# A fused two-layer graph kernel on one core: start-up loads spread over other queues and no longer held back

## The chip, the cores and the metric

The kernel runs on one core of a Trainium2 chip. The metric is device time in microseconds (us) of one execution; the time before is the median of 3 runs.

## What is computed

There are 128 graphs of 128 nodes with 128 features. Layer 0 is a relational graph convolution, of which the fast path of this kernel computes the self-loop relation; layer 1 is a message passing over the same adjacency. Each is followed by a residual addition and a layer norm.

```python
# layer 0, the relation with id 1 (adj_t is adj with nodes swapped)
h = x @ W_loop.T
g = h @ Wg_loop.T
vals = (h + b_loop) * sigmoid(g + bg_loop)
x1 = layernorm(x + relu(onehot(adj_t == 1) @ vals))
# layer 1, relation 1
y = (adj == 1) @ x1 @ weight[0] + bias
out = layernorm(x1 + y)
```

The drawn adjacency has values 0 and 1 only. A general path, which is taken when another value is found, is in the program and is not executed with these inputs.

## The kernel before, in words

The 128 graphs are worked in 32 groups of four. All of a group's tiles are 128 partitions by 512 columns, so one transfer of `x` or of `x_t` for a group is 256 KB, and one transfer of `adj` or `adj_t` for a pair of groups is 512 KB. The program is written engine by engine, with semaphores between them; each engine works through its own list in order.

For group q the steps are:

- **project(q)** on TensorE (line 381): four 128x256 matmuls give `h` and `g` side by side. Each is executed as two passes, so the trace shows eight instructions. They add to bank `hg_ps`, into which ScalarE has first written the bias (`seed`, line 515). For group 0 half of the bias is written by VectorE (line 638).
- **gates(q)** on ScalarE (line 524): sigmoid of `g`. **values(q)** on VectorE (line 727): `h` times gate.
- **loop_sum(q)** on TensorE (line 393): adjacency times `vals`; `first_sum(q)` on VectorE (line 735) adds `x` after the relu, and `first_stats` (line 742) takes the statistics.
- A chain of nine small VectorE operations (lines 665 to 691) makes the reciprocal root; GpSimd then normalises (lines 325 and 333) into `x1`.
- **messages(q)** (line 411) and **message_weights(q)** (line 432) on TensorE, `second_sum` and its statistics on VectorE, the output scaling on ScalarE (line 551), and the store from SyncE.

TensorE's list in step t is project(t), loop_sum(t-1), message_weights(t-5), messages(t-4). VectorE's list in step t is second_sum(t-5) and its statistics, the chain for t, values(t), first_sum(t-1), and the two statistics.

Before the first group there is a start-up. `w_loop_both` (`W_loop` and its transpose) and `wg_loop_t` are loaded, and TensorE multiplies them (line 370, "the fold") so that `h` and `g` come from one product of `x_t` with the 128x256 weight `w_gate`; VectorE copies the product out (line 641, `weights_ready`). Four matmuls on a constant tile `warm` run ahead of the fold (line 367) and two behind it (line 372). VectorE prepares the layer 1 weight from `const_sb` in seven small operations, `message_weight()` (lines 647 to 656). After the sixth, `w1_mid` reaches 3, which is what TensorE's small matmul at line 441 waits for; that matmul stands between project(1) and loop_sum(0) in TensorE's list.

The loads come from three queues. ScalarE's queue has the two loop weights alone. SyncE's queue has `wg_t`, then `xt_sb` and `x_sb` in turn, six buffers of each. GpSimd's queue has the gate bias, the constants, and all of the adjacency, four pairs of each kind. The hold-backs in the lists of SyncE and GpSimd are these:

```python
sp.wait_ge(xt_in[0], 16)      # line 266, ahead of x_t of group 2
sp.wait_ge(xt_in[1], 16)      # line 268, ahead of x of group 1
sp.wait_ge(adj_in[0], 16)     # line 270, ahead of x_t of group 3
pool.wait_ge(xt_in[1], 16)    # line 341, ahead of adjacency pair 1
```

Of the kernel before, what the change touches and what calls it, by code (L numbers as in the profile page):

```python
# [56 lines left out]
    return ((t - FIRST_CHAIN) // 2 + 1) * CHAIN_OPS  # L57


def build(nc, x, x_t, adj, adj_t, w_loop_both, wg_loop_t, gate_bias, consts,  # L60
          w_rel_t, wg_rel_t, b_rel, bg_rel, w_msgs, rel_ids, out):
    with ExitStack() as ctx:
        def sb(name, shape, dt):
# [2 lines left out]
        def sem(name):  # L66
            return ctx.enter_context(nc.semaphore(name))
# [72 lines left out]
        adjt_in = [sem(f"adjt_in{j}") for j in range(ADJ_RING)]  # L140
        out_st = [sem(f"out_st{j}") for j in range(OUT_RING)]
        fold_in = sem("fold_in")
        consts_in = sem("consts_in")
        bias_in = sem("bias_in")
        share_ready = sem("share_ready")
# [76 lines left out]
        def arrived(q, ring):  # L222
            return 16 * (q // ring + 1)
# [18 lines left out]
        def _(sp):  # L242
            def load_xt(q):
                if exists(q):
                    await_count(sp, hg_done, q - XT_RING + 1)
                    sp.dma_start(xt_sb[:, q % XT_RING, :], x_t[q]).then_inc(xt_in[q % XT_RING], 16)
# [12 lines left out]
                    sp.dma_start(out[q], out_sb[:, q % OUT_RING, :]).then_inc(out_st[q % OUT_RING], 16)  # L259

            sp.dma_start(wg_t[:, :], wg_loop_t).then_inc(fold_in, 16)
            load_xt(0)
            load_xt(1)
            load_x(0)

            sp.wait_ge(xt_in[0], 16)
            load_xt(2)
            sp.wait_ge(xt_in[1], 16)
            load_x(1)
            sp.wait_ge(adj_in[0], 16)  # L270
            load_xt(3)
            load_x(2)
            load_xt(4)
# [28 lines left out]
        def _(pool):  # L302
# [32 lines left out]
                            r[:, b:b + 1], n[:, b:b + 1], ALU.mult, ALU.add)  # L335
                    last.then_inc(x1_done, 1)

            pool.dma_start(gate_b[:, :], gate_bias).then_inc(bias_in, 16)
            pool.dma_start(const_sb[:, :], consts).then_inc(consts_in, 16)
            load_adj(0)  # L340
            pool.wait_ge(xt_in[1], 16)
            load_adj(1)
            load_adjt(0)
            load_adj(2)
# [17 lines left out]
        def _(pe):  # L362
# [5 lines left out]
            last.then_inc(marked, 1)  # L368
            pe.wait_ge(fold_in, 16 * 2)
            nc.tensor.matmul(aux_ps[:, 0:P], w_loop, wg_t[:, :], start=True, stop=True).then_inc(fold_done, 1)  # L370
            for _ in range(2):
                nc.tensor.matmul(msg_ps[:, :], warm[:, :], warm_wide, start=True, stop=True)
            pe.wait_ge(weights_ready, 1)
            pe.wait_ge(seeded_dve, 1)

# [9 lines left out]
            def loop_sum(q):  # L385
                if exists(q):
                    spot = q // 2 % ADJ_RING * 2 + q % 2
                    pe.wait_ge(adj_in[q // 2 % ADJ_RING], arrived(q // 2, ADJ_RING))
                    pe.wait_ge(vals_done, q + 1)

                    await_count(pe, s_done, q)
                    for b in range(GB):
                        last = nc.tensor.matmul(loop_ps[:, batch(b)], adj_sb[:, spot, batch(b)],  # L393
                                                vals[:, q % 2, batch(b)], start=True, stop=True)
                    last.then_inc(loop_done, 1)
# [104 lines left out]

        @block.scalar
        def _(act):
            act.dma_start(w_all[:, 0:2 * P], w_loop_both).then_inc(fold_in, 16)
            act.wait_ge(table_ready, 1)
            nc.scalar.activation(table[:, :], half[:, :], ACT.Sigmoid)

# [48 lines left out]
            def look(q):  # L555
                if exists(q):
                    spot = q // 2 % ADJ_RING
                    act.wait_ge(adj_in[spot], arrived(q // 2, ADJ_RING))

                    await_count(act, seen_done, q)  # L560
                    nc.scalar.activation(seen[:, :], adj_sb[:, 2 * spot + q % 2, :], ACT.Square, bias=half[:, 0:1],  # L561
                                         accum_out=seen_sum[:, q:q + 1]).then_inc(seen_done, 1)
# [64 lines left out]
        def _(dve):  # L627
# [4 lines left out]
            nc.vector.memset(stats[:, :, :, :].rearrange("p a c d -> p (a c d)"), 0.0)  # L632
            nc.vector.memset(ones[:, :], 1.0)
            nc.vector.memset(share[:, :], 1.0 / P).then_inc(share_ready, 1)

            dve.wait_ge(marked, 1)
            dve.wait_ge(bias_in, 16)
            nc.vector.tensor_copy(hg_ps[:, 0, 2:4, :], gate_b[:, None, :].broadcast_to([P, 2, 2 * P]))\  # L638
                .then_inc(seeded_dve, 1)
            dve.wait_ge(fold_done, 1)  # L640
            nc.vector.tensor_copy(w_all[:, 2 * P:3 * P], aux_ps[:, 0:P]).then_inc(weights_ready, 1)  # L641

            def message_weight():

# [158 lines left out]
                dve.wait_ge(odd_ready, 1)  # L803
                ts(odd[:, :], worst[:, :], W / 4 + 0.5, None, ALU.is_gt).then_inc(odd_ready, 1)

            message_weight()
            for t in range(GROUPS + 1):
                steps = chain(t)

                def step(n):  # L810
                    for _ in range(n):
                        next(steps, None)

                if exists(t - Z_LAG):
                    second_sum(t - Z_LAG)
                    step(1)
                    second_stats(t - Z_LAG, 0)
                    step(1)
                    second_stats(t - Z_LAG, 1)
                    step(2)  # L820
                else:
                    step(CHAIN_OPS)
                if exists(t):
                    values(t)
                step(1)
                if exists(t - LOOP_LAG):
                    first_sum(t - LOOP_LAG)
                    step(2)
                    first_stats(t - LOOP_LAG, 0)
                    step(1)  # L830
                    first_stats(t - LOOP_LAG, 1)
                step(CHAIN_OPS)
                if t == 1:
                    message_weight_end()
# [137 lines left out]
```

## Time and profile before

| | |
|---|---|
| median of 3 runs | 167.06 us (166.71 to 167.41) |
| the profiled execution, its own time | 167.7 us |
| its span (first to last instruction) | 166.0 us |
| TensorE matmul busy | 153.1 us, 92% of the span |
| VectorE busy | 145.5 us, 88% |
| ScalarE busy | 126.2 us, 76% |
| GpSimd busy | 79.9 us, 48% |
| DMA | 42.76 MB, mean 258 GB/s |

The profiled execution took 1.7 us more than its span, for what lies around it, and its own time is 0.64 us above the median. All times of single instructions in this document are of that execution, in us from the start of the span. In the rows PE is TensorE's matmul, PEld its weight load, DVE is VectorE, ACT ScalarE, POOL GpSimd and SP SyncE; a q behind the name means the engine's sequencer or its DMA queue. "x8" behind a row means eight instructions merged.

### The profile page before, as it was taken

Reading aid. Unit: us, or ns where it says so; the run is one execution under the profiler, and the core shown is the slowest. Engines: PE = TensorE matmul, PEld = TensorE weight load, DVE = VectorE, ACT = ScalarE, POOL = GpSimd, SP = SyncE. Lnnn points to the kernel's source line nnn. Section 1 sums busy time; section 2 is a strip of 40 time slices with the busy share of each in tenths; the row PEclk is TensorE's granted clock in tenths of the full one; section 3 lists DMA queues with packets and bytes.
Section 4 is the critical chain, followed back from the end, with each engine's and each line's share of the span. In section 5 each row is a group of like instructions: output and inputs, shape, how many; then the busy total and the mean of one; then the engine's idle time right before and its main releaser. Section 6 shows DMA issues by size and latency. Waiting matters only on the chain.

```text
span 166.0 us, 3902 instructions
## 1 busy us (share of the span) xinstructions
PE 153.1 (92%) x1068; PEld 141.9 (85%) x1068; DVE 145.5 (88%) x583; ACT 126.2 (76%) x287; POOL 79.9 (48%) x194
## 2 busy tenths in 40 slices
PE   6499899999999999999999999999999999998910
PEld 2278789999999999999999999999999999997910
DVE  1425999999999999999999999999999999999770
ACT  3318767679988888888888888899888887754670
POOL 4070456264737474747466464646374544446000
PEclk9999999999999999999999999999999999999996
DMA  4999999989598979798998979797979261131133
GB/s 123 332 300 315 396 399 396 391 281 321 153 300 288 380 222 348 275 310 308 285 348 245 374 224 381 211 371 206 370 243 360 31 226 39 41 117 63 67 124 139
DMA packets 18857, 42.76 MB, mean 258 GB/s; under 512 B 2112, under 2 KB 2368, under 8 KB 18832
## 3 DMA queue, kind: packets, MB, share of 16 engines
q1 hardware_dynamic: 13968, 25.24, 42.3%
q0 software_dynamic: 4720, 17.11, 33.8%
q8 instruction: 10, 0.16, 0.4%
q14 instruction: 15, 0.12, 0.2%
q10 hardware_dynamic: 144, 0.13, 0.2%
HBM read 34.08 MB, written 8.39 MB: 256 GB/s over the span
## 4 chain that ended last, share of the span: by engine, by line
PE 85%; DVE 5%; issue 3%; DMA 3%; ACT 1%; ACTq 0%; DVEq 0%; POOLq 0%
PE hg_ps L381 33%; PE msg_ps L411 16%; PE loop_ps L393 15%; PE y_ps L432 15%; DMA gate_b<-gate_bias_dram 3%; PE hg_ps L432 2%; PE hg_ps L428 2%; DVE s_sb L735 1%; ACT gate L524 1%; PE y_ps L428 1%; PE hg_ps L411 1%; ACT out_sb L551 1%; DVE stats L742 0%; DVE hg_ps L638 0%; DVE z_sb L753 0%
## 5 line engine op out<-in xcount | busy, mean ns | idle before, releaser
L381 PE MATMUL hg_ps<-w_all,xt_sb 128*128 128x256 f32 x256 | 63.3, 393 | 2.2 <-DVE w_all L641 2.2
L333 POOL TENSOR_SCALAR x<-s_sb,rstd,nmr 128x128 f32<-128x128 f32 x125 | 55.0, 452 | 3.5 <-issue 0.2
L381 PEld LDWEIGHTS hg_ps<-w_all,xt_sb 128*128 128x128 f32 x256 | 48.2, 198 | 8.9 <-DVE w_all L641 3.1
L515 ACT ACTIVATE hg_ps<-gate_b 128x1024 f32<-128x1024 f32 (+1 forms) x32 | 32.0, 1002 | 9.6 <-DVE vals L727 6.0
L551 ACT ACTIVATE out_sb<-z_sb,rstd 128x128 f32<-128x128 f32 x112 | 38.0, 392 | 0.3 <-DVE rstd L691 0.2
L325 POOL TENSOR_TENSOR nmr<-mean_neg,rstd 128x4 f32<-128x4 f32 x31 | 6.2, 201 | 63.6 <-DVE rstd L691 63.6
L393 PEld LDWEIGHTS loop_ps<-vals,adj_sb 128*128 128x128 f32 x256 | 33.3, 192 | 2.7 <-issue 1.3
L393 PE MATMUL loop_ps<-vals,adj_sb 128*128 128x128 f32 x256 | 33.9, 275 | 0.5 <-DVE s_sb L735 0.5
L411 PE MATMUL msg_ps<-adjt_sb,x 128*128 128x128 f32 x248 | 33.0, 276 | 0.0
L524 ACT ACTIVATE gate<-hg_ps 128x512 f32<-128x512 f32 x32 | 19.1, 596 | 17.0 <-PE hg_ps L381 16.8
L432 PE MATMUL y_ps<-w,msg_t 128*128 128x128 f32 x232 | 30.7, 275 | 0.0
L411 PEld LDWEIGHTS msg_ps<-adjt_sb,x 128*128 128x128 f32 x248 | 30.2, 192 | 0.1
L432 PEld LDWEIGHTS y_ps<-w,msg_t 128*128 128x128 f32 x232 | 28.2, 192 | 0.0
L727 DVE TENSOR_TENSOR vals<-hg_ps,gate 128x512 f32<-128x512 f32 x32 | 22.0, 689 | 6.0 <-ACT gate L524 5.0
L742 DVE BATCH_NORM_STATS2 stats<-s_sb 128x6 f32<-128x256 f32 x64 | 26.5, 426 | 0.3
L757 DVE BATCH_NORM_STATS2 stats<-z_sb 128x6 f32<-128x256 f32 x56 | 23.7, 427 | 0.0
L561 ACT ACTIVATE seen<-adj_sb,half 128x512 bf16<-128x512 f32 x32 | 22.8, 711 | 0.1
L735 DVE SCALAR_TENSOR_TENSOR s_sb<-loop_ps,x_sb 128x512 f32<-128x512 f32 x32 | 21.8, 682 | 0.0
L534 ACT ACTIVATE msg_t<-msg_ps 128x512 f32<-128x512 f32 x31 | 18.0, 580 | 4.0 <-PE msg_ps L411 4.0
L753 DVE TENSOR_TENSOR z_sb<-y_ps,x 128x512 f32<-128x512 f32 x28 | 19.1, 683 | 0.0
L308 POOL DMA_DIRECT2D adj_sb<-adj_dram x16 | 9.4, 588 | 4.9 <-DMA xt_sb<-x_t_dram 4.9
L315 POOL DMA_DIRECT2D adjt_sb<-adj_t_dram x16 | 8.7, 545 | 0.0
(66 smaller groups left out, 103.8 us busy)
## 6 DMA issues: line engine op xcount, KB each, us to landing
xt_sb<-x_t_dram SPq DMA_DIRECT2D x32, 256.0 KB, 6.3
x_sb<-x_dram SPq DMA_DIRECT2D x32, 256.0 KB, 6.4
adj_sb<-adj_dram POOLq DMA_DIRECT2D x16, 512.0 KB, 4.5
adjt_sb<-adj_t_dram POOLq DMA_DIRECT2D x16, 512.0 KB, 6.7
out<-out_sb SPq DMA_DIRECT2D x32, 256.0 KB, 3.9
const_sb<-consts_dram POOLq DMA_DIRECT2D x1, 192.0 KB, 5.0
w_all<-w_loop_both_dram ACTq DMA_DIRECT2D x1, 128.0 KB, 2.3
gate_b<-gate_bias_dram POOLq DMA_DIRECT2D x1, 128.0 KB, 4.9
```

What stands on the lines that cost most here:

```text
L333: last = nc.gpsimd.tensor_scalar(x1[:, q % X1_RING, batch(b)], s_sb[:, q % S_RING, batch(b)], r[:, b:b + 1], n[:, b:b + 1], ALU.mult, ALU.add)
L381: last = nc.tensor.matmul(hg_ps[:, q % 2, b, :], xt_sb[:, q % XT_RING, batch(b)], w_gate, start=False, stop=True, skip_group_check=True)
L393: last = nc.tensor.matmul(loop_ps[:, batch(b)], adj_sb[:, spot, batch(b)], vals[:, q % 2, batch(b)], start=True, stop=True)
L411: last = nc.tensor.matmul(msg_of(q)[:, batch(b)], x1[:, q % X1_RING, batch(b)], adjt_sb[:, spot, batch(b)], start=True, stop=True)
L432: last = nc.tensor.matmul(y_of(q)[:, batch(b)], msg_t[:, q % 2, batch(b)], w1[:, :], start=q < LAST, stop=True, skip_group_check=q >= LAST)
L515: nc.scalar.activation(hg_ps[:, q % 2, 0:graphs, :], gate_b[:, None, :].broadcast_to([P, graphs, 2 * P]), ACT.Copy).then_inc(seeded, 1)
L551: last = nc.scalar.activation(out_sb[:, q % OUT_RING, batch(b)], src, ACT.Copy, scale=r)
L561: nc.scalar.activation(seen[:, :], adj_sb[:, 2 * spot + q % 2, :], ACT.Square, bias=half[:, 0:1], accum_out=seen_sum[:, q:q + 1]).then_inc ...
L727: tt(vals[:, q % 2, :].rearrange("p (b n) -> p b n", b=GB), hg_ps[:, q % 2, :, 0:P], gate[:, q % 2, :].rearrange("p (b n) -> p b n", b=GB) ...
L735: stt(s_sb[:, q % S_RING, :], loop_ps[:, :], 0.0, x_sb[:, q % X_RING, :], ALU.max, ALU.add)\
L742: got = nc.vector.bn_stats(stats[:, (q + NORM1_LAG) % STATS_RING, p, :], s_sb[:, q % S_RING, 2 * p * P:2 * (p + 1) * P].rearrange("p (i n) ...
L757: got = nc.vector.bn_stats(stats[:, (q + STAT2_LAG) % STATS_RING, 2 + p, :], z_sb[:, q % Z_RING, 2 * p * P:2 * (p + 1) * P].rearrange("p ( ...
```

## The change

It does six things to the start-up and leaves the groups' work as it was.

1. The gate bias and the constants are loaded from ScalarE's queue, behind `W_loop`, and no longer from GpSimd's.
2. `w_loop_both` is split: `W_loop` (64 KB) on ScalarE's queue, its transpose (64 KB) second on SyncE's queue, with a semaphore of its own, `w_gate_in`, that TensorE waits for ahead of project(0).
3. GpSimd's queue has the adjacency alone. The first pair goes in two transfers of 256 KB, and the readers of group 0 wait for the first of them (`first_adj`).
4. All four hold-backs are taken out, so that twelve loads of `x_t` and `x` and seven of the adjacency are issued with nothing to wait for.
5. There are three `warm` matmuls behind the fold where there were two.
6. VectorE copies the folded weight ahead of its half of the bias, and `message_weight()` is moved from ahead of the groups to behind values(0).

```diff
             sp.dma_start(wg_t[:, :], wg_loop_t).then_inc(fold_in, 16)
+            sp.dma_start(w_all[:, P:2 * P], w_loop_t).then_inc(w_gate_in, 16)
             load_xt(0)
             load_xt(1)
             load_x(0)
-            sp.wait_ge(xt_in[0], 16)
             load_xt(2)
-            sp.wait_ge(xt_in[1], 16)
             load_x(1)
-            sp.wait_ge(adj_in[0], 16)
             load_xt(3)
...
-            pool.dma_start(gate_b[:, :], gate_bias).then_inc(bias_in, 16)
-            pool.dma_start(const_sb[:, :], consts).then_inc(consts_in, 16)
-            load_adj(0)
-            pool.wait_ge(xt_in[1], 16)
+            pool.dma_start(adj_sb[:, 0, :], adj[0, :, 0:W]).then_inc(first_adj, 16)
+            pool.dma_start(adj_sb[:, 1, :], adj[0, :, W:2 * W]).then_inc(adj_in[0], 16)
             load_adj(1)
...
-            for _ in range(2):
+            for _ in range(3):
                 nc.tensor.matmul(msg_ps[:, :], warm[:, :], warm_wide, start=True, stop=True)
+            pe.wait_ge(w_gate_in, 16)
             pe.wait_ge(weights_ready, 1)
             pe.wait_ge(seeded_dve, 1)
...
-            act.dma_start(w_all[:, 0:2 * P], w_loop_both).then_inc(fold_in, 16)
+            act.dma_start(w_all[:, 0:P], w_in).then_inc(fold_in, 16)
+            act.dma_start(gate_b[:, :], gate_bias).then_inc(bias_in, 16)
+            act.dma_start(const_sb[:, :], consts).then_inc(consts_in, 16)
...
+            dve.wait_ge(fold_done, 1)
+            nc.vector.tensor_copy(w_all[:, 2 * P:3 * P], aux_ps[:, 0:P]).then_inc(weights_ready, 1)
             dve.wait_ge(marked, 1)
             dve.wait_ge(bias_in, 16)
             nc.vector.tensor_copy(hg_ps[:, 0, 2:4, :], gate_b[:, None, :].broadcast_to([P, 2, 2 * P]))\
                 .then_inc(seeded_dve, 1)
-            dve.wait_ge(fold_done, 1)
-            nc.vector.tensor_copy(w_all[:, 2 * P:3 * P], aux_ps[:, 0:P]).then_inc(weights_ready, 1)
...
-            message_weight()
             for t in range(GROUPS + 1):
...
                 if exists(t):
                     values(t)
+                if t == 0:
+                    message_weight()
                 step(1)
```

In `loop_sum` on TensorE and in `look` on ScalarE, group 0 waits for `first_adj` and every other group for `adj_in` as before.

VectorE's list at the start, before the change; `hg_ps<-gate_b` is the bias, `w_all<-aux_ps` the folded weight, and the rows on `mid_stat`, `mid`, `b_mid` and `const_sb` are `message_weight()`:

```order
L638 COPY hg_ps<-gate_b 128x512 [waits bias_in,marked]
L641 COPY w_all<-aux_ps 128x128 [waits fold_done]
L647 BN_STATS mid_stat<-const_sb 128x6 [waits consts_in]
L648 BN_STATS mid_stat<-const_sb 128x6
L650 BN_AGGR mid<-mid_stat 128x2 [waits w1_mid]
L651 BN_AGGR mid<-mid_stat 128x2
L653 TENSOR_SCALAR b_mid<-const_sb,mid 128x128 [waits w1_mid]
L654 TENSOR_SCALAR const_sb<-const_sb,mid 128x128
L656 TENSOR_TENSOR b_mid<-b_mid,const_sb 128x128 [waits w1_mid]
L727 TENSOR_TENSOR vals<-hg_ps,gate 128x512 [waits gate_done] x2
```

The same stretch of the changed kernel:

```order
L643 COPY w_all<-aux_ps 128x128 [waits fold_done]
L647 COPY hg_ps<-gate_b 128x512 [waits bias_in,marked]
L734 TENSOR_TENSOR vals<-hg_ps,gate 128x512 [waits gate_done]
L654 BN_STATS mid_stat<-const_sb 128x6 [waits consts_in]
L655 BN_STATS mid_stat<-const_sb 128x6
L657 BN_AGGR mid<-mid_stat 128x2 [waits w1_mid]
L658 BN_AGGR mid<-mid_stat 128x2
L660 TENSOR_SCALAR b_mid<-const_sb,mid 128x128 [waits w1_mid]
L661 TENSOR_SCALAR const_sb<-const_sb,mid 128x128
L663 TENSOR_TENSOR b_mid<-b_mid,const_sb 128x128 [waits w1_mid]
L734 TENSOR_TENSOR vals<-hg_ps,gate 128x512 [waits gate_done]
```

The two copies have changed places, and the seven rows of `message_weight()` now stand between values(0) and values(1).

SyncE's list of loads at the start, before the change:

```order
L261 DMA wg_t<-wg_loop_t_dram 128x128
L246 DMA xt_sb<-x_t_dram 128x512 x2
L251 DMA x_sb<-x_dram 128x512
L246 DMA xt_sb<-x_t_dram 128x512 [waits xt_in0]
L251 DMA x_sb<-x_dram 128x512 [waits xt_in1]
L246 DMA xt_sb<-x_t_dram 128x512 [waits adj_in0]
```

The same stretch of the changed kernel:

```order
L263 DMA wg_t<-wg_loop_t_dram 128x128
L264 DMA w_all<-w_loop_t_dram 128x128
L248 DMA xt_sb<-x_t_dram 128x512 x2
L253 DMA x_sb<-x_dram 128x512
L248 DMA xt_sb<-x_t_dram 128x512
L253 DMA x_sb<-x_dram 128x512
```

One load of 64 KB stands ahead of the first `x_t`, and the three waits are gone.

## Rows read from the trace of the kernel before

**Rows 1.** The page: busy time by engine, the 40 slices, the chain that ended last.
```profile
PE 153.1 (92%) x1068; PEld 141.9 (85%) x1068; DVE 145.5 (88%) x583; ACT 126.2 (76%) x287; POOL 79.9 (48%) x194
...
PE   6499899999999999999999999999999999998910
...
PE 85%; DVE 5%; issue 3%; DMA 3%; ACT 1%; ACTq 0%; DVEq 0%; POOLq 0%
```

**Rows 2.** The chain in order of time, 0 to 30: start us, us, what.
```profile
1.39 4.89 DMA gate_b<-gate_bias_dram
...
6.39 0.69 DVE hg_ps L638
...
7.33 6.50 PE hg_ps L381 x16
...
18.97 0.69 DVE s_sb L735
...
19.80 1.13 PE loop_ps L393 x8
...
21.86 1.73 PE hg_ps L381 x8
```

**Rows 3.** The timeline to 16: start us, us, engine, line, operation.
```profile
0.87 0.40 ACTq L503 DMA_DIRECT2D w_all<-w_loop_both_dram  x1
...
1.31 1.28 ACT L505 ACT_TABLE_LOAD   x1 [1.31 <-PEq L964]
...
3.45 0.80 PE L370 MATMUL aux_ps<-wg_t,w_all 128*128 128x128 f32 x2 [0.36 <-DMA wg_t<-wg_loop_t_dram]
...
4.04 1.06 PE L372 MATMUL msg_ps<-warm 128*128 128x512 bf16 x2
6.38 1.54 ACT L515 ACTIVATE hg_ps<-gate_b 128x512 f32<-128x512 f32 x2 [3.57 <-DMA gate_b<-gate_bias_dram]
...
7.19 0.28 DVE L647 BATCH_NORM_STATS2 mid_stat<-const_sb 128x6 f32<-128x128 f32 x1
...
8.18 0.28 DVE L654 TENSOR_SCALAR const_sb<-const_sb,mid 128x128 f32<-128x128 f32 x1
...
11.15 0.60 ACT L524 ACTIVATE gate<-hg_ps 128x512 f32<-128x512 f32 x1 [3.22 <-PE hg_ps L381]
...
11.78 0.69 DVE L727 TENSOR_TENSOR vals<-hg_ps,gate 128x512 f32<-128x512 f32 x1 [2.98 <-ACT gate L524]
...
13.44 0.41 PEld L441 LDWEIGHTS aux_ps<-const_sb,share 128*128 128x128 f32 x2
...
15.09 0.68 DVE L735 SCALAR_TENSOR_TENSOR s_sb<-loop_ps,x_sb 128x512 f32<-128x512 f32 x1
```

**Rows 4.** The timeline of PE alone, 8 to 11.
```profile
7.33 4.21 PE L381 MATMUL hg_ps<-w_all,xt_sb 128*128 128x256 f32 x9 [2.23 <-DVE w_all L641]
```

**Rows 5.** Windows, 10 to 13: busy us and instructions by engine, PEclk, DMA share, GB/s.
```profile
10.00:13.00 3.00, 3.00 (x8) 2.36 (x7) 0.69 (x1) 1.10 (x2) 1.30 (x3) 1.00 0.97 312
```

**Rows 6.** The loads of x_t of groups 0 and 1: min/median/max to landing.
```profile
L246 SPq DMA_DIRECT2D xt_sb<-x_t_dram x2: 421/422/424, 1.3 to 1.8; - x2
...
DMA to landing us min/median/max: 2.7/4.4/6.0
```

**Rows 7.** The loads of x_t of group 3 and of group 4.
```profile
L246 SPq DMA_DIRECT2D xt_sb<-x_t_dram x1: 328/328/328, 9.3 to 9.3; - x1
...
DMA to landing us min/median/max: 7.5/7.5/7.5
...
L246 SPq DMA_DIRECT2D xt_sb<-x_t_dram x1: 948/948/948, 10.2 to 10.2; - x1
...
DMA to landing us min/median/max: 10.5/10.5/10.5
```

**Rows 8.** The load of x of group 1.
```profile
L251 SPq DMA_DIRECT2D x_sb<-x_dram x1: 328/328/328, 7.9 to 7.9; - x1
...
DMA to landing us min/median/max: 6.1/6.1/6.1
```

More of the change, by code:

```diff
@@ L57, in chain_end, with build @@
     return ((t - FIRST_CHAIN) // 2 + 1) * CHAIN_OPS
-def build(nc, x, x_t, adj, adj_t, w_loop_both, wg_loop_t, gate_bias, consts,
+def build(nc, x, x_t, adj, adj_t, w_in, w_loop_t, wg_loop_t, gate_bias, consts,
           w_rel_t, wg_rel_t, b_rel, bg_rel, w_msgs, rel_ids, out):
@@ L142, in build @@
         fold_in = sem("fold_in")
+        w_gate_in = sem("w_gate_in")
+        first_adj = sem("first_adj")
         consts_in = sem("consts_in")
@@ L387, in loop_sum @@
                     spot = q // 2 % ADJ_RING * 2 + q % 2
-                    pe.wait_ge(adj_in[q // 2 % ADJ_RING], arrived(q // 2, ADJ_RING))
+                    if q == 0:
+                        pe.wait_ge(first_adj, 16)
+                    else:
+                        pe.wait_ge(adj_in[q // 2 % ADJ_RING], arrived(q // 2, ADJ_RING))
                     pe.wait_ge(vals_done, q + 1)
@@ L557, in look @@
                     spot = q // 2 % ADJ_RING
-                    act.wait_ge(adj_in[spot], arrived(q // 2, ADJ_RING))
+                    if q == 0:
+                        act.wait_ge(first_adj, 16)
+                    else:
+                        act.wait_ge(adj_in[spot], arrived(q // 2, ADJ_RING))
                     await_count(act, seen_done, q)
@@ L948 @@
         "adj_t": grouped(adj.transpose(0, 2, 1), 2 * GB),
-        "w_loop_both": _np.concatenate([w["L0_gnn_W_loop"], w["L0_gnn_W_loop"].T], axis=1),
+        "w_loop": _np.ascontiguousarray(w["L0_gnn_W_loop"]),
+        "w_loop_t": _np.ascontiguousarray(w["L0_gnn_W_loop"].T),
         "wg_loop_t": _np.ascontiguousarray(w["L0_gnn_Wg_loop"].T),
```

## The prediction

> **What bounds the kernel now.** I read the page first. TensorE's matmuls are busy for 92% of the span, its slices are full from the third on, and 85% of the chain that ended last is TensorE [rows 1]. The change touches no group's work, so the question is only when TensorE's full stretch begins, and for that I read the chain in order of time [rows 2]. The reader is to see three pieces in it. Up to 6.39 it is one transfer, the gate bias, which is issued at 1.39 and lands 4.89 later; then VectorE's copy of it, and at 7.33 TensorE begins projections 0 and 1. From 13.8 to 19.8 it runs over VectorE, with first_sum(1) at 18.97 and 0.69 long as its last piece. From 19.80, loop_sum(2), it is TensorE to the end. So the end moves by as much as loop_sum(2) moves, provided the loads keep up, and loop_sum(2) stands 4.71 behind first_sum(0), which begins at 15.09 [rows 2, 3]. I take those 4.71 us over unchanged. The sum therefore asks: when does first_sum(0) begin after the change?
>
> TensorE runs the first projections at half pace. The first nine passes of line 381 take 4.21 [rows 4], the first of them longer than the rest: with 0.80 for it the other eight take 0.43 each. Later eight passes take 1.73, or 0.22 each [rows 2]. These are the paces of 1.2 and of 2.4 GHz, though the granted clock reads 1.00 here too [rows 5], so I go by durations. All sixteen passes took 6.50; after nine of them 2.29 are left for seven, and that comes out with about four slow and three fast ones. The pace changed near 13.1, after 5.8 us of work without a gap. The work before it (fold and warm matmuls from 3.45, the last ending at 5.10, then nothing to 7.33 [rows 3]) did not bring the change.
>
> **The change part by part, up to project(0).**
>
> - *Gate bias on ScalarE's queue.* It is issued behind W_loop, whose issue starts at 0.87 and takes 0.40 [rows 3], so at 1.27. From the hardware queues I have 2.7 for the first x_t and 6.0 for the second [rows 6]; on GpSimd's queue it took 4.89 [rows 2]. Half of the first x_t's size, with 64 KB ahead of it, it is nearest to the 2.7: landing at 4.0. By 4.89 it would be 6.2.
> - *The copies.* The fold ends at 3.45 + 0.80 = 4.25 [rows 3]; the weight copy now comes first and is done by 4.6. Then the bias copy, 0.69 [rows 2]: 5.3. ScalarE's seed is no later; its table load of 1.28 [rows 3] starts two issues (0.8) later and ends near 3.4, under the wait for the bias.
> - *Third warm matmul.* Two took 1.06 from 4.04 [rows 3], so three end at 5.63. It costs nothing while something else ends later; if both bias and x_t were there at 5.3 it would cost 0.3.
> - *W_loop's transpose.* 64 KB, issued at 1.3, ahead of x_t on SyncE's queue. In the trace W_loop and the other weight of about this size are in by 3.45, when the fold starts [rows 3]. It will be there with x_t at the latest.
> - *The first x_t.* It is issued one issue (0.42) later, at 1.74, which is just where the second was issued before. Its bounds are the 2.7 of the first and the 6.0 of the second [rows 6]: landing from 4.4 to 7.8. The first had 64 KB ahead of it on its queue, the second 320 KB; now 128 KB are ahead, but ScalarE's queue carries 384 KB in place of 128. I take a little under the middle, 4.3, and land it at 6.0. This is the term I trust least.
>
> So project(0) starts at 6.0, not 7.33, and x_t decides it.
>
> **From project(0) to first_sum(0).** TensorE now works from 3.45 with a gap of under 0.4 us. I let the pace change 5.8 us after that start, at 9.25. All slow, project(0) would take 0.80 + 7 x 0.43 = 3.8 and end at 9.8; about 1.3 passes of it become fast and it ends at 9.5 (before, 11.1). Behind it come the gate, 0.60, and values(0), 0.69, with the handovers: before, 11.1 to 12.47 [rows 3], or 1.35. So values(0) ends at 10.9. Project(1) takes 1.73 and ends at 11.25.
>
> Now the moved message_weight() counts. Before, it ran from 7.19, while VectorE had nothing else, and its sixth operation, which TensorE's line 441 waits for, ended at 8.18 + 0.28 = 8.46 [rows 3]: 1.27 after its start, and free. Now it starts when values(0) ends: 10.9 + 0.05 + 1.27 = 12.2. TensorE stands before line 441 from 11.25, about 1 us idle. From the weight load of line 441 to first_sum(0) it was 13.44 to 15.09, or 1.65 [rows 3], and it stays so: first_sum(0) at 13.85. Without the move first_sum(0) would follow project(1) as before (13.83 to 15.09, 1.26) and begin at 12.5. The gain is 15.09 - 13.85 = **1.25 us**.
>
> **The loads behind it, costed at nothing.** Taking out the hold-backs makes GpSimd's queue full from the first microseconds, and it stays so for seven transfers. What it does to SyncE's queue the trace shows for the later time when both were full: x of group 1, issued at 7.85, landed 6.1 later at 13.95 [rows 8]; x_t of group 3 at 16.8; x_t of group 4, two transfers behind it, at 20.7 [rows 7]. That is 2.85 and then 1.95 us for each 256 KB. At 1.95, x_t of group 1 lands at 8.0 (wanted 9.5), of group 2 at 11.9 (wanted about 13.7), of group 3 five transfers behind the first, at 15.75. Loop_sum(2) is now due at 18.55, so project(3), 1.73, has to start by 16.8. That holds, by 1 us only. The first adjacency transfer has half the bytes of the one before and stands first on its queue; it is wanted at 12.5 and is there. The constants are wanted at 10.9, third on ScalarE's queue. The end of the kernel is untouched.
>
> The Trainium skill (DMA: Bandwidth & Descriptors, "Issuing engines are not separate DMA queues") says that transfers from all engines share the same DMA engines and that spreading them saves only issue time. No row contradicts a shared total: it is 312 GB/s in the busy stretch of rows 5. By that rule taken strictly the bias would still need about its 4.89 us, and the sum would be the one of the second rival below.
>
> **Sum.** 1.25 us off an execution of 167.7 gives 166.45. The profiled execution is 0.64 above the median, so the median should go from 167.06 to **165.8**. A measurement can tell about 0.5% (0.84 us) from no change.
>
> **The rivals.**
>
> 1. *GpSimd's queue starves SyncE's (slower).* If 2.85 us per transfer, the first spacing in rows 7 and 8, holds for the whole start, x_t of group 3 lands at 6.0 + 5 x 2.85 = 20.25. Project(3) ends at 22.0 and loop_sum(2) starts there, 2.2 later than the 19.80 of before: 169.3. Against it is the 1.95 of the next two transfers, and that GpSimd's initial list is finite. It decides from a spacing of 2.16 on, begins to eat the gain there, and makes the kernel slower than before from 2.4 on. Chance of slower by over 0.5%: 0.12. A further 0.08 eats most of the gain only.
> 2. *The transfers come no earlier (no change).* With the bias landing 4.89 after 1.27, project(0) starts at 6.2 + 0.7 = 6.9, and with x_t at its other bound, at 7.8. From 7.33 or later, with the pace changing no sooner than in my sum or not at all, the gain is 0.5 or less: 166.6 to 167.2. Chance 0.15.
> 3. *The pace changes earlier.* TensorE had a second stretch of work, from 1.20 to 3.1, before the fold. If the change needs less than 5.8 us of nearly unbroken work, it could be there at 6.0. Then project(0) takes 0.6 + 7 x 0.22 = 2.1, ends at 8.1, and first_sum(0) begins at 8.1 + 4.3 = 12.4: gain 2.7, or 164.4. For it speaks that nothing in the row shows how much is needed; against it, that the work before 5.10 brought nothing and that the second x_t would be late. Chance 0.17.
>
> **How the numbers follow.** My own case has 0.48, its range is x_t at 4.4 to 7.0, which is 165.2 to 166.6 (start no sooner than 5.65, by the third warm matmul). Faster by over 0.5%: nearly all of rival 3 and most of my case, 0.66 together. Slower: rival 1 with 0.12. Within 0.5%: the rest, 0.22. The range goes from rival 3's value to just past no change, **164.4 to 167.1**, which leaves out rival 1's slower side and a little at the fast end.
>
> **What would show it.** The step is right if line 381 begins near 6.0 with x_t, not the bias, as what it waited for; if values(0) is followed by seven small VectorE operations while TensorE waits at line 441's successor for about 1 us; if loop_sum(2) starts near 18.55 with VectorE's first_sum as its releaser. It is wrong if TensorE waits for a transfer at project(1), (2) or (3), or if the passes of project(0) are already at 0.22.

## The result and the profile after

The changed kernel took 167.94 us (median of 20 runs, 166.53 to 169.89); the kernel before, beside it, 166.97 us (20 runs). The ratio is 1.0073, with a 95% interval from 1.0047 to 1.0100. It is slower by 0.7%, where I forecast 0.7% faster, and outside my range. The profiled execution took 168.34 us with a span of 166.7; before, 167.7 and 166.0.

The page of the changed kernel, the lines that answer to [rows 1]:

```profile
PE 153.7 (92%) x1069; PEld 141.8 (85%) x1069; DVE 146.7 (88%) x583; ACT 126.3 (76%) x287; POOL 78.9 (47%) x193
...
PE   6399999999999999999999999999999999998910
...
PE 84%; DVE 6%; DMA 4%; issue 2%; ACT 1%; SPq 0%; ACTq 0%; DVEq 0%
```

Nothing has changed in the body; the second slice has lost one tenth. The chain in order of time shows where, beside [rows 2] (start us, us, what):

```profile
1.79 5.91 DMA xt_sb<-x_t_dram
7.70 0.25 issue
7.95 3.77 PE hg_ps L380 x8
...
12.37 0.69 DVE vals L734
...
14.31 0.49 PE aux_ps L443 x2
14.80 0.91 PE loop_ps L395 x8
15.73 0.70 DVE s_sb L742
...
19.62 0.69 DVE s_sb L742
20.45 1.13 PE loop_ps L395 x8
```

The chain no longer begins with the bias but with `x_t` of group 0, which lands at 7.70. Project(0) starts at 7.95, not 7.33; loop_sum(2) at 20.45, not 19.80, or 0.65 later; and the span is 0.7 us longer. As I had read from the trace before, the end moves by as much as loop_sum(2). The medians are 0.97 us apart, since the two profiled executions stand 0.73 and 0.40 above theirs. One execution of either kernel can stand 1 us or more from its median, so a difference of this size between two traces says where the time went, and only the ratio says what it is worth.

The start of the timeline of the changed kernel, beside [rows 3] (start us, us, engine, line, operation):

```profile
1.31 0.46 ACTq L506 DMA_DIRECT2D gate_b<-gate_bias_dram  x1
1.32 0.42 SPq L264 DMA_DIRECT2D w_all<-w_loop_t_dram  x1
...
1.79 0.90 SPq L248 DMA_DIRECT2D xt_sb<-x_t_dram  x2
1.80 0.45 ACTq L507 DMA_DIRECT2D const_sb<-consts_dram  x1
...
3.78 1.49 PE L370 MATMUL msg_ps<-warm 128*128 128x512 bf16 x3
3.92 1.54 ACT L519 ACTIVATE hg_ps<-gate_b 128x512 f32<-128x512 f32 x2
...
4.24 0.69 DVE L647 COPY hg_ps<-gate_b 128x512 f32<-128x512 f32 x1
...
7.95 6.27 PE L380 MATMUL hg_ps<-w_all,xt_sb 128*128 128x256 f32 x16 [2.68 <-DMA xt_sb<-x_t_dram]
```

The bias gained what it was meant to gain: its seed runs at 3.92 in place of 6.38, and by 4.93 both halves of the bank are ready. Then TensorE, done with its third warm matmul at 5.27, stands idle for 2.68 us until `x_t` is there. In the changed kernel the two relevant loads took (min/median/max to landing, the bias first, then `x_t` of groups 0 and 1):

```profile
DMA to landing us min/median/max: 2.5/2.5/2.5
...
DMA to landing us min/median/max: 5.9/6.4/6.9
```

Before, `x_t` of group 0 had taken 2.7 [rows 6]. So the question became: what, of the six things that the change does, makes that load land 3.7 us later?

### The profile page after: what moved, and what is told of

The parts are those of the page before. It is cut to its first block, busy times and chain, and to the rows that moved or that the text cites. A ratio compares the mean times of both kernels' runs of the same rounds, so it can differ in the third digit from the quotient of the medians.

```text
span 166.7 us, 3906 instructions
## 1 busy us (share of the span) xinstructions
PE 153.7 (92%) x1069; PEld 141.8 (85%) x1069; DVE 146.7 (88%) x583; ACT 126.3 (76%) x287; POOL 78.9 (47%) x193
## 4 chain that ended last, share of the span: by engine, by line
PE 84%; DVE 6%; DMA 4%; issue 2%; ACT 1%; SPq 0%; ACTq 0%; DVEq 0%
PE hg_ps L380 31%; PE msg_ps L413 16%; PE loop_ps L395 16%; PE y_ps L434 15%; DMA xt_sb<-x_t_dram 4%; PE hg_ps L434 2%; PE hg_ps L430 2%; DVE s_sb L742 1%; ACT gate L528 1%; PE y_ps L430 1%; PE hg_ps L413 1%; ACT out_sb L555 1%; DVE vals L734 1%; DVE stats L749 0%; DVE z_sb L760 0%
## 5 line engine op out<-in xcount | busy, mean ns | idle before, releaser
L675 DVE TENSOR_SCALAR tiny<-tiny 128x8 int32<-128x8 int32 x34 | 9.0, 266 | 0.2
L307 POOL DMA_DIRECT2D adj_sb<-adj_dram x15 | 8.9, 591 | 0.0
```

## The experiments

All ratios are to the kernel before, measured beside each on the same chip. "Landing" is that of `x_t` of group 0; "start" is the first pass of project(0). Three of the columns come from one profiled execution each. The rows were measured on several chips, and the median of the kernel before beside them was 166.97 for the changed kernel, 166.84 for e1 to e8, 166.72 for e9 to e12 and 167.14 for e13 to e16. So medians of different rows can be 0.4 us apart for the chip alone, and where it matters I compare the ratios.

| | differs from | median us | ratio (95%) | landing | start | loop_sum(2) |
|---|---|---|---|---|---|---|
| before | | | 1 | 4.0 | 7.33 | 19.80 |
| changed | | 167.94 | 1.0073 (1.0047 to 1.0100) | 7.7 | 7.95 | 20.45 |
| e1 | changed, holds back | 167.66 | 1.0057 (1.0023 to 1.0092) | 7.1 | 7.36 | 18.72 |
| e2 | changed, adjacency waits | 166.95 | 0.9996 (0.9968 to 1.0024) | 6.2 | | |
| e11 | e2 again | 167.03 | 1.0036 (0.9999 to 1.0073) | 5.8 | 6.06 | 18.72 |
| e3 | changed, one weight load | 165.91 | 0.9940 (0.9911 to 0.9969) | 4.3 | 5.43 | 18.65 |
| e4 | changed, preparation early | 167.61 | 1.0052 (1.0027 to 1.0078) | 8.2 | 8.42 | 21.07 |
| e10 | changed, transpose behind | 167.53 | 1.0038 (1.0006 to 1.0070) | 4.9 | 7.79 | 20.54 |
| e13 | changed, constants on GpSimd's | 167.00 | 0.9991 (0.9965 to 1.0018) | 6.9 | 7.17 | 19.08 |
| e8 | before, bias alone | 165.74 | 0.9920 (0.9887 to 0.9953) | 4.4 | 5.62 | 17.85 |
| e9 | e8 and split | 165.87 | 0.9941 (0.9909 to 0.9973) | 6.4 | 6.66 | 18.03 |
| e14 | e8 and no holds | 165.92 | 0.9921 (0.9893 to 0.9949) | 4.4 | 5.69 | 18.69 |
| e15 | e8 and constants | 166.21 | 0.9938 (0.9915 to 0.9961) | 4.6 | 5.83 | 17.98 |
| e16 | e8 and third warm | 165.66 | 0.9898 (0.9864 to 0.9932) | 4.7 | 5.99 | 18.05 |
| e5 | e3 and holds | 165.87 | 0.9938 (0.9909 to 0.9966) | 4.3 | 5.37 | 20.00 |
| e6 | e3, preparation early, one hold | 165.97 | 0.9946 (0.9913 to 0.9979) | 4.3 | 5.44 | 18.08 |
| e7 | e6, adjacency paced | 165.55 | 0.9916 (0.9887 to 0.9944) | 4.2 | 5.33 | 17.37 |
| e12 | e7, less pacing | 166.19 | 0.9975 (0.9951 to 0.9999) | 4.4 | 5.54 | 18.43 |

In every one of these traces the span ends 145.6 to 146.5 us after loop_sum(2) starts (145.6 in e5, 145.9 or more in the others). That column therefore says what one execution won or lost. It is one execution, though: e1's was the fastest of its twelve and e4's the slowest. The median is the verdict.

### Undoing parts of the changed kernel

e1 puts the hold-backs back.

```diff
+            sp.wait_ge(xt_in[0], 16)
             load_xt(2)
+            sp.wait_ge(xt_in[1], 16)
             load_x(1)
+            sp.wait_ge(adj_in[0], 16)
             load_xt(3)
...
+            pool.wait_ge(xt_in[1], 16)
             load_adj(1)
```

> The changed kernel with its four hold-backs put back and nothing else undone. In the changed kernel x_t of group 0, issued at 1.79, lands at 7.7 and project(0) starts at 7.95. Theory A (GpSimd's queue, when it begins to move near 3.2, stops SyncE's queue, and x_t of group 0 is no longer through by then): x_t of group 0 has its first competitors unchanged, so it still lands at 7 or later and the time stays within 0.4 us of the changed kernel. Theory B (the weight transpose, bias and constants ahead of it and beside it on the hardware queues take its time): the same as A. Theory C (the freed prefetch takes its bandwidth): it lands by 5, project(0) starts below 6, and the time falls by 1.2 us or more.

Measured: landing at 7.1 and 167.66 us, within 0.3 of the changed kernel. Theory C falls. The freed prefetch is at most 0.6 us of the 3.7, and that is within what one execution differs from another: e4 below, whose early loads are those of the changed kernel, has the landing at 8.2, and e2 and e11, one kernel twice, have 6.2 and 5.8.

e2 and e11 hold GpSimd's first load until `x_t` of group 0 has landed.

```diff
+            pool.wait_ge(xt_in[0], 16)
             pool.dma_start(adj_sb[:, 0, :], adj[0, :, 0:W]).then_inc(first_adj, 16)
```

> The changed kernel, with GpSimd's first adjacency load held until x_t of group 0 has landed. Theory A: x_t of group 0 lands near 4.5, project(0) starts at 5.5 to 6, and the time falls by 1.2 us or more, to about 166.7, unless the adjacency, now issued some 3 us later, comes late for loop_sum(0). Theory B: x_t of group 0 still lands at 6.5 or later and the time stays within 0.5 us of the changed kernel. Theory C: no change either, since the freed prefetch of SyncE is still there.

> e2 once more, for its profile: in e2's profiled execution TensorE ran at a fifth of its speed throughout and its stages can't be read, though the loads can: x_t of group 0 issued at 1.79 landed 4.4 later, where the changed kernel has 5.9. I expect the same landing near 6.2, project(0) at 6.3 to 6.6 in place of 7.95, the adjacency in time for loop_sum(0), and a time about 1 us under the changed kernel, as e2's median of 166.95.

In e2's profiled execution the passes of project(0) and (1) took about 1.35 us each and the span was 888.6 us, for a reason that no run shows, so only its loads were read, and e11 repeats the kernel. In the timeline of e11, TensorE alone, and for `x_t` of group 0:

```profile
6.06 6.15 PE L381 MATMUL hg_ps<-w_all,xt_sb 128*128 128x256 f32 x16 [0.80 <-DMA xt_sb<-x_t_dram]
12.42 0.49 PE L444 MATMUL aux_ps<-const_sb,share 128*128 128x128 f32 x2 [0.20 <-DVE const_sb L662]
...
18.72 1.13 PE L396 MATMUL loop_ps<-vals,adj_sb 128*128 128x128 f32 x8 [0.41 <-DVE s_sb L743]
...
DMA to landing us min/median/max: 4.0/4.0/4.0
```

With GpSimd's queue silent the load still takes 4.0 us, not the 2.7 of before, but 1.9 less than in the changed kernel (in e2's profile it took 4.4, or 1.5 less). So theory A has a part: the adjacency beside it makes 1.5 to 1.9 of the 3.2 us by which the load takes longer. The rest I put on the hardware queues (B); e3 and e13 bear on it. The two medians agree to 0.1 us while their ratios, 0.9996 and 1.0036, differ by 0.4%, which shows what the comparison can tell apart. e2 is clear of the changed kernel's 1.0073; e11's interval overlaps it.

e3 takes the weight's transpose off SyncE's queue.

```diff
-            sp.dma_start(w_all[:, P:2 * P], w_loop_t).then_inc(w_gate_in, 16)
...
-            act.dma_start(w_all[:, 0:P], w_in).then_inc(fold_in, 16)
+            act.dma_start(w_all[:, 0:2 * P], w_loop_both).then_inc(fold_in, 16)
```

> The changed kernel, with both halves of the loop weight again in one load on ScalarE's queue, so that only 64 KB stand ahead of x_t of group 0 on SyncE's queue and it is issued near 1.3. Theory A: it may just get through before GpSimd's queue moves at 3.2, as it did before the change (landing at 4.0); then project(0) starts below 6 and the time falls by 1.2 us. Theory B: it gets back the part that the 64 KB took, 1 to 2 us of landing, and the time falls by 0.5 to 1.2 us. Theory C: no change.

Measured: landing at 4.3, start at 5.43, and 2.0 us off the changed kernel: the largest effect of all, more than either theory gave it, and the kernel is now faster than before. Its timeline, TensorE alone:

```profile
5.43 1.97 PE L378 MATMUL hg_ps<-w_all,xt_sb 128*128 128x256 f32 x8 [0.21 <-DVE hg_ps L645]
...
8.96 1.99 PE L378 MATMUL hg_ps<-w_all,xt_sb 128*128 128x256 f32 x8 [1.57 <-DMA xt_sb<-x_t_dram]
...
12.87 1.99 PE L378 MATMUL hg_ps<-w_all,xt_sb 128*128 128x256 f32 x8 [0.80 <-DMA xt_sb<-x_t_dram]
...
16.82 1.99 PE L378 MATMUL hg_ps<-w_all,xt_sb 128*128 128x256 f32 x8 [1.06 <-DMA xt_sb<-x_t_dram]
```

And its window from 10 to 13, beside [rows 5]:

```profile
10.00:13.00 3.00, 2.20 (x16) 1.91 (x15) 2.10 (x6) 1.95 (x4) 0.00 (x0) 1.00 1.11 399
```

Two things are to be seen. The passes of project(0) take 0.25 us from the first, so the fast pace (2.4 GHz) was there at 5.43, as rival 3 had it. And once the first load is early, the next bound shows: `x_t` of the following groups lets project start at 8.96, 12.87 and 16.82, 3.9 us apart. Between two of them SyncE's queue carries one `x_t` and one `x`, so a load of 256 KB takes 1.95 us there, while all queues together move 399 GB/s. That is the spacing of rows 7 and 8 and rival 1's mechanism; it takes back part of the gain and not more. TensorE's waits for these loads are 3.6 us in all (the fourth, of 0.17, is at 20.77).

e10 leaves all bytes where they are and exchanges two lines.

```diff
-            sp.dma_start(w_all[:, P:2 * P], w_loop_t).then_inc(w_gate_in, 16)
             load_xt(0)
+            sp.dma_start(w_all[:, P:2 * P], w_loop_t).then_inc(w_gate_in, 16)
```

> The changed kernel with two lines of SyncE exchanged: x_t of group 0 is issued first, at 1.32, and the 64 KB of the weight transpose behind it. The bytes on the queues by the time of project(0) are the same. Theory S: x_t of group 0 lands near 4.3 as in e3; the transpose, now at 1.74, is what project(0) waits for, landing anywhere from 5 to 7.5, so the time falls by 0.3 to 1.5 us against the changed kernel, and TensorE waits for x_t of the later groups as in e3. If only the number of bytes counted and not which load is first, project(0) would still start near 7.9.

The first line is of TensorE's timeline in e10, the second of its loads of `w_all` (W_loop and its transpose), the third of its load of `x_t`:

```profile
7.79 6.76 PE L380 MATMUL hg_ps<-w_all,xt_sb 128*128 128x256 f32 x16 [2.56 <-DMA w_all<-w_loop_t_dram]
...
DMA to landing us min/median/max: 2.0/4.0/6.0
...
DMA to landing us min/median/max: 3.6/3.6/3.6
```

`x_t` lands at 4.9, and now the 64 KB of the transpose, issued at 1.8, take 6.0 us. SyncE's first load is `wg_t`, the second is issued at 1.3, the third at 1.8. The third is the late one here. Before and in e8 the third is `x_t` of group 1, which nobody wants yet; in e3 it is the same load, and TensorE waits 1.57 us for it. In the changed kernel project(0) needs all of the first three. I had written that with equal bytes the start would stay near 7.9 if only the bytes counted; it did stay (7.79), and yet the order did matter for each load by itself. What hardly changes is when the later of the two is in. With it SyncE's queue has moved 384 KB in both kernels, so e10 can't tell the place in the queue from the bytes that have to pass. It does show that a load's own size is not what makes it late.

e13 takes the constants off the hardware queues.

```diff
-            act.dma_start(const_sb[:, :], consts).then_inc(consts_in, 16)
...
+            pool.dma_start(const_sb[:, :], consts).then_inc(consts_in, 16)
             pool.dma_start(adj_sb[:, 0, :], adj[0, :, 0:W]).then_inc(first_adj, 16)
```

> The changed kernel with the constants alone back on GpSimd's queue, first there. Theory K (192 KB of constants on the hardware queues beside x_t of group 0 push it from e9's 6.4 to 7.7): it lands by 6.6, project(0) starts near 6.7, and the time falls by 1 us to about 166.9. Theory F (the freed prefetch does it): it stays above 7.2 and the time within 0.4 us of the changed kernel.

For `x_t` of group 0 in e13, and TensorE's timeline:

```profile
DMA to landing us min/median/max: 5.1/5.1/5.1
...
7.17 5.38 PE L381 MATMUL hg_ps<-w_all,xt_sb 128*128 128x256 f32 x16 [2.30 <-DMA xt_sb<-x_t_dram]
```

The landing comes 0.8 us earlier and the median falls by 0.9 us, as theory K said, though to 6.9 and not 6.6. The 0.8 is little more than the 0.5 by which e4's landing differs from the changed kernel's; the ratio, 0.9991 against 1.0073, is clear. The constants are the second part of the loss.

e4 puts VectorE's preparation back ahead of the groups.

```diff
+            message_weight()
             for t in range(GROUPS + 1):
...
-                if t == 0:
-                    message_weight()
```

> The changed kernel, with the seven VectorE operations that prepare the layer 1 weight back ahead of the groups, where VectorE idles from 4.9 on. In the changed kernel TensorE waits 0.49 us for the sixth of them. All theories of the transfer say the same: project(0) stays near 7.95; first_sum(0) comes 0.25 to 0.5 us earlier, and the time falls by that, 0.2 to 0.5 us.

The median fell by 0.3 us, the ratio from 1.0073 to 1.0052, with intervals that overlap. It is inside what was expected and not shown. In e4's trace first_sum(0) starts 1.26 us after the end of project(1), as before the change; in the changed kernel it is 1.51. In the changed kernel TensorE waited 0.49 us before the weight load of line 443, but project(1)'s last pass ended only at 14.22, 0.09 before it.

### Single parts on the kernel before

e8 moves the bias alone.

```diff
-            pool.dma_start(gate_b[:, :], gate_bias).then_inc(bias_in, 16)
...
             act.dma_start(w_all[:, 0:2 * P], w_loop_both).then_inc(fold_in, 16)
+            act.dma_start(gate_b[:, :], gate_bias).then_inc(bias_in, 16)
```

> The kernel before, with the gate bias alone moved to ScalarE's queue behind its weight load; the constants and the adjacency stay on GpSimd's, now issued 0.7 us sooner, and the hold-backs, the two warm matmuls and VectorE's order stay. It is the part of the change that I costed with a landing at 4.0. If the bias lands by 4.6 and x_t of group 0 still near 4.0 (nothing is added ahead of it), project(0) starts at 5.6 to 5.9 in place of 7.33, and the time falls by 1.0 to 1.7 us. If, as in the changed kernel, x_t is pushed to 6 or later by the load beside it, it falls by less than 0.5.

Measured: start at 5.62 and 0.8% faster than before. This is the gain that I had forecast for the whole change, and it is all in one line of it. Four more kernels add one part each to e8.

> e8 (the kernel before with the bias on ScalarE's queue, 165.74 us) plus the split of the loop weight: its transpose, 64 KB, goes on SyncE's queue ahead of x_t of group 0. Nothing else of the change. Theory S (the split alone takes back what the bias gives): x_t of group 0, in e8 among the first and landing near 4.4, lands at 6 or later, project(0) starts 1 us or more later than e8's 5.62, and the time rises by 0.8 to 2 us against e8, to or above the kernel before. Theory R (it takes the split together with the unheld adjacency and the constants beside it): x_t lands by 5.2 and the time stays within 0.4 us of e8.

> e8 with the constants moved to ScalarE's queue too, and nothing else. x_t of group 0 is issued at 1.32 here, before the constants at 1.8, so it still lands by 4.6 and project(0) starts near 5.6. But VectorE has the layer 1 preparation, which waits for the constants, ahead of values(0): they landed at 8.2 to 9.3 in e3, e6 and e12. If they land after project(0)'s gate, near 9.5, values(0) waits; else nothing. I expect the time within 0.4 us of e8.

> e8 (bias alone on ScalarE's queue, 165.74 us) with all four hold-backs taken out and nothing else. Theory K: x_t of group 0 keeps e8's landing near 4.4 and project(0) its 5.62; x_t of groups 1 and on come 3.9 us apart as in e3, and the time is that of e3 or a little above, 165.7 to 166.3. Theory F: it loses 1 us or more against e8.

> e8 with the third warm matmul and nothing else. Two end near 4.9 and project(0) starts at 5.62, so the third, 0.43 to 0.5 us, fits under the wait for the bias copy. Either nothing (within 0.3 us of e8), or, if the fuller stretch of work brings the faster pace sooner in more of the executions, up to 0.8 us less in the median.

Their edits are those shown for the change. First lines of project(0) in e8, e9, e15 and e16, in this order:

```profile
5.62 6.25 PE L380 MATMUL hg_ps<-w_all,xt_sb 128*128 128x256 f32 x16 [0.53 <-DVE w_all L641]
```

```profile
6.66 5.38 PE L383 MATMUL hg_ps<-w_all,xt_sb 128*128 128x256 f32 x16 [1.97 <-DMA xt_sb<-x_t_dram]
```

```profile
5.83 6.04 PE L379 MATMUL hg_ps<-w_all,xt_sb 128*128 128x256 f32 x16 [0.73 <-DVE w_all L641]
```

```profile
5.99 5.72 PE L380 MATMUL hg_ps<-w_all,xt_sb 128*128 128x256 f32 x16 [0.51 <-DVE w_all L641]
```

The split (e9) moves the landing from 4.4 to 6.4 and makes TensorE wait for `x_t`, as theory S said; but the time rises by only 0.13 us in the median (0.2% in the ratio, with intervals that overlap), which is theory R's figure for the time. In the execution shown the sixteen passes took 5.38 in place of 6.25, so most of the late start was given back by the pace; whether that holds for most executions I can't say from one trace. This much can be said: none of the four parts tried costs more than 0.5 us in the median on top of e8 (e15's 0.47 is just outside the 0.4 that I had expected, and 0.2% in the ratio). The moved preparation, the exchanged copies and the halved first adjacency pair were not tried alone. All together turn 0.8% faster into 0.7% slower. As far as these runs go, the loss is in the combination: the split makes project(0) need the third load of SyncE's queue; the constants and the adjacency beside it, which matter little while `x_t` is the second, then delay just that load to 7.7. Taking away any one of the three, the split (e3), the constants (e13) or the adjacency (e2), brings the kernel back to about the time of before (e2, e11, e13) or under it (e3).

### Looking for a better kernel

These start from e3. e5 has all hold-backs; e6 has the preparation early and only GpSimd's hold; e7 paces GpSimd's loads by the landing of `x_t`; e12 leaves the second half of pair 0 free.

```diff
+            pool.wait_ge(xt_in[1], 16)
             pool.dma_start(adj_sb[:, 1, :], adj[0, :, W:2 * W]).then_inc(adj_in[0], 16)
             load_adj(1)
+            pool.wait_ge(xt_in[2], 16)
             load_adjt(0)
+            pool.wait_ge(xt_in[3], 16)
             load_adj(2)
             load_adjt(1)
```

> e3 (one weight load on ScalarE's queue) plus the four hold-backs put back. In e3 project(0) starts at 5.43, but x_t of groups 1 to 4 land one after the other 3.9 us apart and TensorE waits for each, 3.6 us in all; SyncE's queue gets a third of a full 399 GB/s. Theory H (the unheld adjacency takes what SyncE's queue needs): with the hold-backs x_t of group 1 lands by 8 and the waits shrink to under 1.5 us in all; the time falls by 0.5 us or more against e3. Theory N (hold-backs cost what they save, as e1 showed against the changed kernel): x_t of groups 3 and 4, issued at 9 or later, land near 16.8 and 20.7 as before the change, and the time is within 0.4 us of e3.

> e3, with VectorE's layer 1 weight preparation back ahead of the groups, and with the one hold-back of GpSimd's queue (adjacency pair 1 waits for x_t of group 1); SyncE's loads stay free. Theory H: x_t of groups 1 and 2 land by 8 and 10, the rest earlier than in e3, and the time falls by 0.7 to 1.5 us against e3. Theory N: no change beyond 0.3 us, since by the time of group 3 all the adjacency is issued anyway.

> As e6, with GpSimd's first loads paced by the landing of x_t: the second half of pair 0 and pair 1 after x_t of group 1, adj_t pair 0 after group 2, the rest after group 3. Theory H: TensorE waits for no x_t by more than 0.5 us, loop_sum(2) starts near 17, and the time falls by 1.5 us against e3, to about 164.5. Theory N: as e6, or slower because adj_t of pair 0 is late for messages(0).

> Candidate: e7 with the second half of adjacency pair 0 not held (TensorE waited 0.37 us for it in e7's loop_sum(1)). If that wait was on the path, the time falls by up to 0.4 us under e7's 165.55; if the 256 KB come back to delay x_t of group 1, project(1) waits and the time is that of e6, 165.9.

TensorE's timeline in e5, then in e7:

```profile
16.64 3.57 PE L382 MATMUL hg_ps<-w_all,xt_sb 128*128 128x256 f32 x8 [2.07 <-DMA xt_sb<-x_t_dram]
```

```profile
14.34 1.16 PE L396 MATMUL loop_ps<-vals,adj_sb 128*128 128x128 f32 x8 [0.37 <-DMA adj_sb<-adj_dram]
15.33 1.89 PE L381 MATMUL hg_ps<-w_all,xt_sb 128*128 128x256 f32 x8
17.37 1.13 PE L396 MATMUL loop_ps<-vals,adj_sb 128*128 128x128 f32 x8
```

Against e3, e5 and e6 changed the median by less than 0.1 us, as theory N had it; e7 gained 0.4 where theory H gave 1.5, and its interval overlaps e3's. In e5 SyncE's own hold-backs make `x_t` of group 3 late: project(3) waits 2.07 us and then runs at the slow pace. In e7 no project waits for a load, and loop_sum(2) starts at 17.37, the earliest of all. Of all kernels the best ratios are those of e16 (0.9898), e7 (0.9916), e8 (0.9920) and e14 (0.9921), whose intervals overlap, so pacing the adjacency is not shown to be worth anything over moving the bias alone. e12's expected gain over e7 did not come; it is 0.6 us slower in the median. Its `x_t` of group 1 took 7.2 us where e7's took 6.0, but no project waited for it. What its chain shows is the constants: with the preparation ahead of the groups and the constants third on ScalarE's queue, VectorE waits for them before values(0). They landed at 9.26 in e12, and values(0) started at 10.8; in e7 it was 8.0 and 9.75. In e6 (VectorE's first operation of the preparation) they came late too:

```profile
8.94 0.29 DVE L653 BATCH_NORM_STATS2 mid_stat<-const_sb 128x6 f32<-128x128 f32 x1 [3.60 <-DMA const_sb<-consts_dram]
```

So part of what e6 and e12 lose to e7 is this wait, and not `x_t`. Pacing on top of e8, whose constants come from GpSimd's queue, was not tried.

## Why the prediction was wrong

- **What bounds the kernel, and that the end moves with loop_sum(2): right.** The start decides, and the 4.71 us from first_sum(0) to loop_sum(2) came out as 20.45 - 15.73 = 4.72.
- **Bias landing 4.0, copies 5.3: right.** It was 3.8 (1.31 + 2.5), and the copies ended at 4.93. e8 shows the value of this step alone, 0.8%.
- **Third warm matmul, nothing: right** (e16 against e8, within 0.1 us in the median).
- **"The first x_t ... I take a little under the middle, 4.3, and land it at 6.0": this step failed.** It took 5.9 and landed at 7.7. Both bounds were in the text, 2.7 and 6.0, and the true value is at the upper one, that of the load issued at the same moment before the change. I had weighed kilobytes ahead of it against kilobytes on ScalarE's queue, and left out that GpSimd's queue has the adjacency from 1.4 on. The runs show instead that all three count: the same load took 4.0 and 4.4 with the adjacency held (e11, e2), 5.1 with the constants off ScalarE's queue (e13), and 3.0 with the transpose no longer ahead of it (e3).
- **The landing is not the whole of the miss.** e11 is the changed kernel with `x_t` at 5.8, so it runs the rest of my sum. Project(0) started at 6.06 (my sum: 6.0), first_sum(0) at 14.00 (13.85), loop_sum(2) at 18.72 (18.55), and the execution took 166.7 (166.45). Yet the ratios of this kernel are 0.9996 and 1.0036, not 0.9925. I had read 1.25 us off one execution of the kernel before and taken them off its median. The profiled execution of before is 0.73 above its median of 20 and e11's 0.33 under its own, so the 1.0 us between the two executions is not in the medians. What sets a typical execution apart from the profiled one no run shows. With the landing right, this change measures as no change and not as the gain of my sum.
- **The upper bound was priced on the wrong side.** In rival 2 I let project(0) start at 7.8 and still wrote "the gain is 0.5 or less: 166.6 to 167.2". A start at 7.8 is later than 7.33, so with an unchanged pace it is a loss. With that worked out, slower would have had more than 0.12, and the range, which ended at 167.1, would have gone further up.
- **"I let the pace change 5.8 us after that start, at 9.25": wrong here.** All of project(0) ran slow (eight passes in 3.77), and the sixteen passes took 6.27, 0.2 less than before. It did not hang on the late start alone: with a start at 6.06 (e11) and 5.99 (e16) the eight passes took 3.77 and 3.79 too. Nor does the idle time before them decide it: it was 2.68 us in the changed kernel and 0.80 and 0.51 in those two, while in e9 and e1, after 1.97 and 2.13, the first passes were fast.
- **Moved preparation, 1.35 us (13.85 against 12.5): oversized.** It followed from a start at 6.0 with an early pace. With the late start it cost first_sum(0) 0.25 us: 15.73 against 14.22 + 1.26. With the earlier starts of e11 and e13 it cost 0.53 and 0.55 (14.00 against 12.21 + 1.26, and 14.36 against 12.55 + 1.26), so it may be part of what keeps these two at the time of before. e4 can't tell its undoing from nothing, and it was not undone where it costs more.
- **Freed loads at nothing: right for the changed kernel, and their spacing of 1.95 us too** (e3). With an early start they do cost: in e14 TensorE waits 0.71 and 1.09 us for `x_t` of groups 2 and 3, and loop_sum(2) starts 0.8 later than in e8, though the ratios are the same. Rival 1, my slower case, did not occur: with the spacing at 1.95 the kernel is still faster than before in e3 and e14.
- **Rival 3, the pace changes earlier: not in the changed kernel, but in e3**, whose passes were fast from 5.43. There the loads behind took the gain back: loop_sum(2) started at 18.65.
- **The rule that spreading over queues saves only issue time** (the Trainium skill, DMA: Bandwidth & Descriptors, "Issuing engines are not separate DMA queues"). For the bias the traces do not agree: 4.9 us on GpSimd's queue, 2.5 to 3.3 on ScalarE's in the changed kernel and in e8. The shared total they bear out: 404 GB/s between 6 and 7 us before the change, 399 in e3's busy window. What the bias won, the loads beside it paid. The constants won nothing by the move: they landed at 7.1 before (5.0 after their issue) and at 7.9 in the changed kernel (6.1).

What stays open: why the third load of SyncE's queue takes 4.6 to 7.2 us beside busy queues while the second takes about 3 (2.7 to 3.6), whether by its place or by the bytes ahead of it; why e9's later start costs so little; and why e11's kernel, with a start 0.6 us earlier than e9's, is no faster than before while e9 is. No run separates them.

## What to carry to other kernels

When a start is gated by several loads, write down for each the place in its queue and what the other queues carry at that moment, not only its bytes. Splitting a load so that the critical one moves one place back cost it 2 us here (4.4 in e8, 6.4 in e9), and more with each queue that was filled beside it. And before a gain read from one trace is taken off the median, look at how far that trace's own execution stands from the median. Take the one part that shortens the measured chain (here the bias, one line) and measure it alone before adding companions that each look free.

## What I had not expected of the hardware

- A load's time depended more on what stood ahead of it and beside it than on its size: 64 KB took 6.0 us as the third load of SyncE's queue (e10) and 2.1 as the second (changed), 256 KB took 2.7 to 3.6 as the second (before, e10). Both count: as the third, 256 KB took 4.6 us in e9, with 128 KB ahead of it, and 7.2 in e8, with 320 KB.
- The pace of the first projections differs between the profiled executions, each of another kernel; whether it differs between executions of one kernel, no run shows. The sixteen passes of projects 0 and 1 took 5.38 us in e1, e9 and e13, 5.72 in e16, 6.27 in the changed kernel and 6.76 in e10, and in e3 the eight passes of project(0) took 1.97. In e1, e9 and e13 the first passes were fast (e1: three in 0.89 us), and then the clock fell: in e1 the granted clock is 1.00 from 7 to 8, 0.50 from 9 to 12, which is the level of 1.2 GHz, and 1.00 from 13 on. Where the first passes were slow, as before the change, the column reads 1.00 throughout, so there only the durations tell the level. The page of e1 shows the fall in the third slice:

```profile
PEclk9959999999999999999999999999999999999996
```

- A steady share emerged once all queues were full: in e3 and e14 SyncE's queue got 256 KB through in 1.95 to 2.0 us again and again, which is a third of e3's 399 GB/s.
